# Four shared-expert pieces of the first batch moved from behind the attention into the last turn

## What is computed

```python
h = _layernorm(x) * (1 + ca) + sa
x = x + ga * attention(h, wq, wk, wv, wo)          # softmax over 512 keys, 16 heads
h = _layernorm(x) * (1 + cb) + sb
comb = top 4 of softmax(h @ gate_w.T), normalised  # 32 experts
sh = silu(h @ shared_gate_w.T) * (h @ shared_up_w.T)            # 512 wide
out0 = sigmoid(h @ shared_expert_gate_w.T) * (sh @ shared_down_w.T)
x = x + gb * (out0 + sum over experts of comb * expert(h))      # 96 wide each
```

## Time and profile before

| | |
|---|---|
| time, median of 3 executions | 591.85 us (589.08 to 592.23) |
| profiled execution | 589.51 us, span of the core 587.7 us |
| granted TensorE clock, mean | 0.982 of full |
| busy PE / DVE / ACT / POOL | 95% / 63% / 43% / 35% of the span |
| attention with lead-in | to 330.9 us of the span |
| list behind the attention on PE | 330.9 to 398.5 us |
| expert loop and last sums | from 398.5 us |

### The profile page before, as it was taken

The page is one execution under the profiler, slowest core; times in us unless marked ns, Lnnn a source line. Parts: engine busy times, 40 slices in busy tenths (PEclk is TensorE's granted clock), DMA queues, the critical chain, the costliest instruction groups (busy, mean ns, idle before and its releaser), DMA issues.

```text
span 587.7 us, 10308 instructions
## 1 busy us (share of the span) xinstructions
PE 556.5 (95%) x3102; PEld 308.3 (52%) x3102; DVE 371.3 (63%) x862; ACT 255.0 (43%) x519; POOL 206.6 (35%) x268
## 2 busy tenths in 40 slices
PE   4889999999999999999999999999999998999985
PEld 3453223233333333333443456557798897989664
DVE  6386577778678786788866359645344443433397
ACT  3213536664766647555477431103343443434100
POOL 6200000000030660306631753741666766666400
PEclk9976999999999999999999999999999999999998
DMA  7243117100221231311200588624455655542395
GB/s 232 41 117 120 31 38 214 35 7 17 60 60 37 68 97 51 71 37 64 82 2 10 173 263 236 199 82 127 146 155 160 179 154 148 171 139 46 106 414 196
DMA packets 44004, 67.34 MB, mean 115 GB/s; under 512 B 9371, under 2 KB 32292, under 8 KB 43564
## 3 DMA queue, kind: packets, MB, share of 16 engines
q1 hardware_dynamic: 31984, 45.62, 27.7%
q0 software_dynamic: 7680, 16.87, 8.3%
q10 hardware_dynamic: 4288, 4.20, 2.1%
HBM read 38.93 MB, written 27.51 MB: 113 GB/s over the span
## 4 chain that ended last, share of the span: by engine, by line
PE 81%; DVE 9%; issue 3%; DMA 3%; ACT 1%; POOL 1%; SPq 1%; POOLq 0%; ACTq 0%; DVEq 0%
PE ps L876 23%; PE ps L889 11%; PE ps L1107 8%; PE ps L973 7%; PE ps L1128 6%; PE ps L825 5%; PE ps L967 4%; PE ps L834 3%; PE ps L847 3%; PE ps L1093 3%; PE ps L902 3%; DVE max_q L1220 2%; PE ps L811 2%; DMA results<-y_sb,dest 1%; PE ps L932 1%
## 5 line engine op out<-in xcount | busy, mean ns | idle before, releaser
L1220 DVE TENSOR_REDUCE max_q<-ps 128x1 f32<-128x512 f32 x256 | 163.7, 685 | 71.5 <-PE ps L847 69.6
L703 ACT ACTIVATE probs<-ps 128x512 f32<-128x512 f32 x256 | 138.0, 596 | 100.8 <-PE ps L876 100.5
L847 PE MATMUL ps<-k_rows,q_rows 31*128 31x512 f32 x512 | 148.8, 673 | 2.0 <-DMA k_rows<-qk_raw 2.0
L876 PE MATMUL ps<-q_rows,k_rows 32*128 32x512 f32 x512 | 145.6, 647 | 0.9 <-DVE max_q L1220 0.9
L561 POOL DMA_INDIRECT results<-y_sb,dest x96 | 94.9, 989 | 67.0 <-issue 35.1
L876 PEld LDWEIGHTS ps<-q_rows,k_rows 32*128 32x128 f32 x512 | 41.8, 186 | 70.6 <-ACT probs L703 51.1
L1107 PE MATMUL ps<-up_sb,oT 128*128 x384 | 70.8, 327 | 2.3 <-DVE oT L1582 1.4
L889 PE MATMUL ps<-probs,v_ext 128*32 128x512 f32 x512 | 68.2, 605 | 1.1 <-ACT probs L703 1.1
L1107 PEld LDWEIGHTS ps<-up_sb,oT 128*128 128x128 f32 x384 | 61.3, 190 | 3.3 <-issue 3.2
L1128 PE MATMUL ps<-down_sb,e_hidT 96*128 x192 | 49.8, 382 | 3.6 <-ACT e_hidT L760 3.6
L1582 DVE COPY oT<-ps 128x512 f32<-128x512 f32 x48 | 33.0, 690 | 30.7 <-PE ps L1093 30.1
(11 more groups left out here) (180 smaller groups left out, 676.0 us busy)
## 6 DMA issues: line engine op xcount, KB each, us to landing
xe<-dispatched SPq DMA_DIRECT2D x96, 129.0 KB, 2.2
comb<-results SPq DMA_DIRECT2D x16, 512.0 KB, 9.9
up_sb<-in_up SPq DMA_DIRECT2D x12, 512.0 KB, 4.6
dispatched<-pad_rows SPq DMA_DIRECT2D x33, 129.0 KB, 4.5
down_sb<-in_down SPq DMA_DIRECT2D x4, 768.0 KB, 7.2
x<-in_x ACTq DMA_DIRECT2D x4, 512.0 KB, 5.6
q_rows<-qk_raw SPq DMA_DIRECT2D x64, 32.0 KB, 1.9
k_rows<-qk_raw SPq DMA_DIRECT2D x64, 32.0 KB, 1.9
```

The source lines that it names most:

```text
L703: act.activation(probs[:, u % 8, :], ps[:, st_bank(t.b, g, u), :], ACT.Exp).then_inc(exp_done, 1)
L847: pe.matmul(ps[:, banks[u % len(banks)], :], q_rows[32 * i:32 * i + ONE, b % 2, g, qt * P:(qt + 1) * P], k_rows[32 * i:32 * i + ONE, b % 2 ...
L876: pe.matmul(ps[:, st_bank(b, g, n), :], k_rows[32 * i:32 * i + 32, b % 2, g, kt * P:(kt + 1) * P], q_rows[32 * i:32 * i + 32, b % 2, g, :] ...
L1220: dve.tensor_reduce(max_q[:, g % 2, qt, i:i + 1], ps[:, banks[(16 * g + n) % len(banks)], :], AXX, ALU.max).then_inc(max_done, 1)
```

## The change

The table of the last turn gets four entries at its odd places 1, 7, 9 and 11, and the list behind the attention loses the same four pieces of batch 0. The three `between` functions get the calls that do them there; the positions n at which the last batch's chain stands in the list are not changed, so the pieces ahead of each position are other ones than before.

```diff
-    LAST = {"MAX0": 0, "WO0": 3, "WO1": 5, "MAX1": 8, "HT0": 12, "HT1": 13, "LOG": 15, "MAX2": 16, "RANK": 20}
+    LAST = {"MAX0": 0, "SG0@0": 1, "WO0": 3, "WO1": 5, "SU0@0": 7, "MAX1": 8, "SG1@0": 9, "SU1@0": 11, "HT0": 12, "HT1": 13, "LOG": 15, "MAX2": 16, "RANK": 20}
...
         self.shared += [f"SG0@{B - 1}", f"SG1@{B - 1}"]
+        self.shared = [name for name in self.shared if name not in self.LAST]
...
-            return fin if name in fin.uses else late
+            return fin if name in fin.uses else late if name in late.uses else turns[B - 1]
+
+        def shared_at(t, place):
+
+
+            return [name for name in t.places if name[0] == "S" and t.at(name, place)]
...
                 for g in (1, 3):
                     if t.at(f"MAX{g}", place):
                         negate_max(t, g)
+                for name in shared_at(t, place):
+                    if name[1] == "G":
+                        tanh_gate(0, int(name[2]))
...
             def finish(t):
 
-                for c in range(3):
-                    tanh_gate(0, c)
+                for k in range(2, 5):
+                    tanh_gate(k // 4, k % 4)
                 second_norm(t, range(TJ))
-                tanh_gate(0, 3)
+                tanh_gate(1, 1)
...
                 if t.at("LOG", place):
                     logits(t)
+                for name in shared_at(t, place):
+                    shared(name)
...
             def between(t, place):
 
+                for name in shared_at(t, place - 1):
+                    if name[1] == "G":
+                        shared(name)
+                for name in shared_at(t, place):
+                    if name[1] == "U":
+                        shared(name)
                 if place == 0 and t.post:
                     heads_turned(t.b - 1, 3)
```

More of the change, by code:

```diff
@@ L715, in finish @@
                 logits_out(t)
-                tanh_gate(1, 0)
                 expert_weights(t)
-                for k in range(5, 4 * B - 2):
+                for k in range(6, 4 * B - 2):
                     tanh_gate(k // 4, k % 4)
```

## The result

The changed kernel takes 596.26 us (median of 7 executions, 594.51 to 598.06), the kernel before 591.85 us on the same chip (589.08 to 594.98). The ratio is 1.009, with a 95% interval from 1.0065 to 1.0115. The forecast was 597.4 us, which is +5.6; measured by the medians is +4.4.

What follows compares the result with a forecast made beforehand. PE's order of work was taken to bound the kernel, with expert tiles only 1.7 us ahead of its list. Turn +4.7, earlier experts -1.0 and clock +1.9 made +5.6 us, 597.4 us, range 593.4 to 600.0.

Steps and rivals of the forecast that it cites:

- The turn, +4.7: Last turn of attention: four added pieces cost +4.1 us and a late oT 0.6; bounds +4.1 and +5.3.
- The price of a piece, 1.02 us: Each piece lengthens its pair of places on PE by 1.02 us, read from the query projection in batch 2's turn.
- The extra 0.6 at place 3: Place 3's output projection comes 0.6 us later, because SG0@0's gate product goes ahead of DVE's transpose into oT.
- The routing chain, slots +0.7: DVE's routing behind the attention: slots at 34.4 or 34.5 us instead of 33.8; bounds -0.3 and +2.5.
- The dispatch, taken as 27.75 us throughout: From slots to SP's first expert tile load: 27.75 us, set by POOL and its DMAs, moving the load to 62.3.
- pair 3: Expert tiles turned by PE: at 72.4 us behind the attention instead of 73.4, -1.0 us, before the clock's +1.9.
- The clock, +1.9: Start of the expert loop: PE's idle gap drops the clock to half, delaying pair 3 by 1.9 us; bounds 0 and 3.1.
- The list: PE's list behind the attention: four pieces of 1.73 us leave, 6.9 us; with new waits it is done at 62.3.
- The sum: Whole kernel: +4.7 - 1.0 + 1.9 = +5.6 us, 597.4 us against the median.
- The one in which the list sets the start of the experts: Rival, start of experts: 6.9 us come back less new waits of 1.6; sum -0.6, 591.2 us; chance 0.08.
- the one with an unchanged slow routing: Rival, routing: POOL's scaling meets it wholly, slots +2.5, expert loop 0.8 us late; sum +7.4, 599.3 us; chance 0.12.
- The rival with a full clock: Rival, start of the expert loop: the clock holds, so the sum is +3.7 us, 595.5 us; chance 0.20.

Runs made afterwards that it cites:

- the kernel with places 9 and 11: Changed kernel, but only two pieces moved into the last turn, SG0@0 to place 9 and SU0@0 to place 11; ratio to the kernel before 1.0052.
- The kernel with oT first: Changed kernel, but at place 2 of the last turn DVE turns the heads back into oT ahead of SG0@0's product; ratio to the kernel before 1.0108.
- the chain-early runs: Runs with the last batch's chain moved forward in the list: on the changed kernel 1.0027, with two pieces 0.999 and 0.9983 repeated, on the kernel before 1.0023.
- the two kernels with two pieces and an unmoved chain: Changed kernel with only SG0@0 and SU0@0 moved, to places 7 and 9 (ratio to before 1.0137) or 9 and 11 (1.0052).
- the chain-early kernel: Changed kernel with the last batch's norm transposes, logits, ranks and routing moved forward in the list; ratio to the kernel before 1.0027.
- the kernel with two pieces and the early chain: Changed kernel with only two pieces moved, to places 9 and 11, and the last batch's chain forward in the list; ratio to before 0.999, repeat 0.9983.

## Why the prediction was right

- **The turn, +4.7.** Measured +4.8. The price of a piece, 1.02 us, holds: in the changed kernel, and alone in the kernel with places 9 and 11 (2.1 for two). The extra 0.6 at place 3 was 0.7. Its reason was half of the truth: the bank that the product frees would have held the output projection just as long. It was not seen either that a gate piece at place 7 would cost 1.2 us more; the change puts an up piece there, whose product is ready in time, so this was luck.
- **The routing chain, slots +0.7.** Measured +0.4. The logits came later by the difference of two down pieces against two short ones as worked out (3.6 against 3.4), and POOL's scaling, which began 20.6 us behind the attention (20.3 before), met only the first 2 us of the routing: 4.95 us from 360.22 to 365.17, 5.2 expected.
- **The dispatch, taken as 27.75 us throughout.** This was mis-sized in the profile of the changed kernel: 29.0, of which the waits for earlier indirect DMAs are 2.4. In the others it is between 27.9 and 30.4, and 30.8 in one repeat, with 1.4 to 4.4 us of such waits. With 10.1 us from first load to pair 3, as the prediction's working has it (72.4 - 62.3), the tiles allowed 73.3 instead of 72.4.
- **The clock, +1.9.** It fell as expected, and cost 1.0. The two errors of this and the step before, -0.9 and +0.9, cancelled: pair 3 was expected at +0.9 and came at +1.0. That it came so close is luck. The kernel with oT first has the same work behind the attention, and there the dispatch took 27.9 and the clock 1.4, pair 3 at 73.8.
- **The list.** Expected done at 62.3, measured 61.9, after a wait of 1.67 us for the up product behind the table. None of the 6.9 us taken out of it came back. The 1.73 us for a piece are right from start to start (1.72 in the timeline of the changed kernel), but half of the row's 3.63 us, by which the prediction gives them, is 1.82; that row holds the last matmul's tail.
- **The sum.** +5.6 expected, +4.4 measured by the medians. Up to pair 3 the profile has +5.8. Behind it the loop was taken as unchanged; from pair 3 to the last down piece it took 156.0 to 160.8 us in the eleven profiles compared, so a difference of 1 us in the total says nothing about the terms.
- **The rivals.** The one in which the list sets the start of the experts is refuted by the chain-early runs, and the one with an unchanged slow routing by the slots. The rival with a full clock gave 595.5 us, which is nearer to the measured 596.26 than the forecast's 597.4; the time cannot choose between them. The windows do: the clock was at half.

The Trainium skill says of such a loop ("TensorE: Matmul & The Clock Gate", HAM oscillation) that after a wait for DMA the next matmuls start cold. Here that holds for the 4.82 us ahead of pair 0 in the changed kernel: its four transposes took 1.09 us. In the two kernels with two pieces and an unmoved chain, which waited 2.32 and 2.68 us, pair 0's still took 0.63 us, as in the chain-early kernel with its wait of 0.98; the clock had fallen only at pair 1 (1.11 us), behind a second wait of 1.48 and 1.46 us.

## What to carry to other kernels

Before moving work off the end of an engine's list, look for the second chain that runs beside the list, and count how far it lies behind: here 1.7 us, which caps what 6.9 us of removed work can give. Check what the removal does to the order inside the list, since events fixed at positions get other neighbours. And a work put into a gap holds its buffer until its last reader on another engine is done, so its price depends on when that buffer is next claimed. The same holds for a list that takes its buffers in turn: two pieces fewer, and the last ones hold other banks.

## What the hardware showed that was not expected

The last down piece of this kernel, 32 matmuls in the trace, stands behind a wait of 2.10 us in every profile. In the kernel before and in the changed one (chain, start us, us, what):

```profile
563.75 7.14 PE ps L967 x32
```

```profile
568.77 8.83 PE ps L975 x32
```

Windows of the same work in the two kernels, and in the repeat of the kernel with two pieces and the early chain:

```profile
567.00:571.00 4.00, 4.00 (x21) 3.51 (x20) 3.35 (x5) 0.00 (x0) 0.00 (x0) 1.00 1.04 417
```

```profile
570.00:574.00 4.00, 4.00 (x14) 3.22 (x14) 1.92 (x3) 0.00 (x0) 0.00 (x0) 0.66 1.04 412
```

```profile
563.00:567.00 4.00, 3.09 (x10) 2.59 (x11) 3.79 (x6) 0.00 (x0) 0.00 (x0) 0.75 1.03 400
```

The same work took 7.14 and 8.83 us, with a granted clock of 0.66 in the second, which mixes the two levels. The clock fell here in six of the eleven profiles, and the stretch from the end of the expert loop on PE to the end of the span took 45 us in these and 43.3 in the others. Of the two executions of one and the same kernel (two pieces, 9 and 11, chain early) one kept the full clock here and the other did not, so this is no effect of the change. The expert loop also waits up to 1.3 us for a tile, once, twice or not at all, at places that differ by run. Executions of one kernel spread over some 5 us or more (589.08 to 594.98 for the kernel before), more than the effect of one moved piece; these falls and waits are part of that spread, and how large a part was not measured.
